# Window mask carried inside the score products of the last stage, instead of by products of its own

## The reference, cut to what matters

```
q, k = l2norm(q) * qs, l2norm(k) * ksc      # then rotary tables are applied
# a window of 32 queries sees 64 keys: the window before, and its own
mask = (it < jb) | (it > jb + w) | (jb == -1)
sim  = einsum('bhwie,bhwje->bhwij', bq, bk2) * QK_SCALE
sim  = where(mask, -finfo.max, sim)
out  = einsum('bhwij,bhwje->bhwie', softmax(sim), bv2)
```

## Time and profile before

| | |
|---|---|
| median of 3 runs | 4238.78 us (4233.77 to 4241.29) |
| the profiled execution | 4246.35 us, its span 4244.5 us |
| PE busy | 92% of the span, 48128 products |
| DVE busy | 83% |
| ACT busy | 62% |
| POOL busy | 56% (it has little to do before the last stage) |
| DMA engines | 24% |
| granted TensorE clock, mean | 0.964 of full speed |

### The profile page before, as it was taken

The page is one execution under the profiler, slowest core; times in us unless marked ns, Lnnn a source line. Parts: engine busy times, 40 slices in busy tenths (PEclk is TensorE's granted clock), DMA queues, the critical chain, the costliest instruction groups (busy, mean ns, idle before and its releaser), DMA issues.

```text
span 4244.5 us, 120128 instructions
## 1 busy us (share of the span) xinstructions
PE 3910.8 (92%) x48128; PEld 2747.8 (65%) x48128; DVE 3529.0 (83%) x5537; ACT 2638.6 (62%) x5550; POOL 2381.6 (56%) x2045
## 2 busy tenths in 40 slices
PE   3457999999995999999999999999999999999998
PEld 1225776767764676667766676667766676667666
DVE  6875556777776899989998899989998899989897
ACT  3543336666664666666667666666666666666665
POOL 0111001000003787878888788878888787878785
PEclk7678999999997999999999999999999999999999
DMA  3000000000001333333332333333332333333332
GB/s 104 0 0 1 1 1 1 1 0 0 0 1 40 76 90 82 69 76 88 78 78 65 79 88 81 70 75 94 73 81 62 81 87 81 71 73 72 91 77 65
DMA packets 264482, 238.94 MB, mean 56 GB/s; under 512 B 31524, under 2 KB 260136, under 8 KB 263208
## 3 DMA queue, kind: packets, MB, share of 16 engines
q1 hardware_dynamic: 263976, 231.82, 23.5%
HBM read 26.20 MB, written 4.19 MB: 7 GB/s over the span
## 4 chain that ended last, share of the span: by engine, by line
PE 73%; DVE 12%; ACT 7%; issue 3%; SPq 2%; POOL 1%; DMA 1%; DVEq 0%; ACTq 0%; POOLq 0%
PE bank L1977 14%; PE bank L1910 13%; PE bank L1995 8%; PE bank L1950 7%; PE bank L2037 5%; PE bank L854 5%; ACT arena L1129 3%; PE bank L2050 2%; PE bank L1943 2%; DVE arena L1016 2%; PE bank L1921 2%; DVE arena L1026 2%; PE bank L1254 1%; SPq L2151 1%; PE bank L1245 1%
## 5 line engine op out<-in xcount | busy, mean ns | idle before, releaser
L1448 DVE TENSOR_TENSOR arena<-bank,tab 128x1024 f32<-128x1024 f32 x768 | 935.5, 1219 | 193.0 <-ACT arena L1680 138.8
L1835 POOL TENSOR_TENSOR arena<-arena 128x512 f32<-128x512 f32 x768 | 1010.7, 1332 | 49.6 <-DMA arena<-arena 44.9
L1680 ACT ACTIVATE arena<-bank 128x512 f32<-128x512 f32 x768 | 457.9, 596 | 538.9 <-PE bank L1910 530.1
L1977 PE MATMUL bank<-m_vo,arena 128*32 128x512 f32 x6144 | 757.9, 599 | 17.4 <-DVE arena L1541 11.1
L1910 PE MATMUL bank<-x_split,wqk_split 128*128 128x256 f32 x4608 | 720.7, 299 | 34.9 <-DVE arena L1448 21.0
L1910 PEld LDWEIGHTS bank<-x_split,wqk_split 128*128 128x128 f32 x4608 | 605.6, 192 | 184.3 <-issue 93.9
L1843 POOL TENSOR_TENSOR arena<-arena 128x256 f32<-128x256 f32 x768 | 558.6, 739 | 159.4 <-ACT arena L1680 158.7
L1704 ACT ACTIVATE arena<-bank 128x512 f32<-128x512 f32 x768 | 456.8, 596 | 186.9 <-PE bank L1977 184.2
L1852 POOL TENSOR_TENSOR arena<-arena 128x1024 f32<-128x1024 f32 x192 | 372.4, 1940 | 263.2 <-DVE arena L1496 263.2
L1187 POOL TENSOR_TENSOR x_all<-x_all,arena 128x256 f32<-128x256 f32 x16 | 11.6, 727 | 836.5 <-DVE arena L1008 836.5
L1858 POOL TENSOR_TENSOR arena<-arena 128x1024 f32<-128x1024 f32 x192 | 373.5, 1946 | 127.0 <-DVE arena L1509 126.7
(11 more groups left out here) (258 smaller groups left out, 7159.4 us busy)
## 6 DMA issues: line engine op xcount, KB each, us to landing
arena<-arena SPq DMA_DIRECT2D x1536, 128.0 KB, 2.5
wqk_stage<-in_wqk SPq DMA_DIRECT2D x6, 1024.0 KB, 8.6
out_x<-x_all SPq DMA_DIRECT2D x7, 512.0 KB, 6.0
wvt<-in_wvt SPq DMA_DIRECT2D x6, 512.0 KB, 4.4
wo<-in_wo SPq DMA_DIRECT2D x6, 512.0 KB, 5.5
arena<-in_wbh SPq DMA_DIRECT2D x1, 2048.0 KB, 9.7
w<-in_w SPq DMA_DIRECT2D x6, 341.0 KB, 5.9
wqk_stage<-out_x SPq DMA_DIRECT2D x2, 512.0 KB, 5.0
```

The lines of the kernel that those rows point to most:

```text
L1448: nc.vector.tensor_tensor(d_t[c % KS].rearrange("p k h t -> p k (h t)"), bank[c % 2][:, :].unsqueeze(1).to_broadcast([P, 2, 2 * T]), tab[: ...
L1680: nc.scalar.activation(d_sq[i % 4].rearrange("p h t -> p (h t)"), bank[c % 2][:, :], ACT.Square).then_inc(s_sq, 1)
L1835: nc.gpsimd.tensor_tensor(d_rot[i // 4][:, i % 4, :, :], t[:, :, 0, :], t[:, :, 1, :], ALU.add).then_inc(s_ad, 1)
L1977: last = nc.tensor.matmul(bank[U_BANK[w]][g * WIN:(g + 1) * WIN, :], d_xt[n % 3][:, w * WIN:(w + 1) * WIN], m_vo[:, 4 * g:4 * g + 4, :].re ...
```

## The change

It takes the mask products away and puts the mask where the zeros of the keys and the unused half of the queries were. `d_q` gets one more axis, `d_q[:, a, g, z, t]`: the 64 partitions of head `z` hold its queries, and the other 64 hold an identity repeated over the tokens (one-hot rows). In `d_k[:, a, g, z, t]` the 64 partitions that were zero hold rows of the mask. A product over all 128 partitions then gives scores plus mask, but it now serves one head alone, so each product of 128 columns becomes two of 64 columns, each with weights of its own.

- `scores`: for each bank 32 products of 64 columns, `start=True`; no products with `mask_bf`; for the first sequence one more wait, on `s_sel`.
- `mask_rows_d`, new, at the start of GpSimd's last stage: the two memsets that were there, and ten copies that write the one-hot rows and the mask rows, each waited for. PE and ACT no longer wait for these memsets before their loops (`ZEROS` 5 instead of 7). `place_keys` waits for all twelve.
- The four VectorE copies that made `ident_bf` and `mask_bf` at the start of the program go. The mask is loaded into `mask_rows`, which stays.
- `place_queries`: the same eight DMAs, to another address.
- `d_q` has twice its size. For this `d_wf` shares memory with `d_v`, and `d_xc` with `d_r`, and `ffn_square` waits for `s_xc` of the sequence before.

```
-        d_q = ld(2, 4, T)
+        d_q = ld(2, 4, 2, T)
...
-        d_xf, d_v, d_r, d_wf, d_xc, d_xn = ld(T), ld(T), ld(T), ld(T), ld(T), ld(T)
+        d_xf, d_v, d_r, d_xn = ld(T), ld(T), ld(T), ld(T)
+        d_wf, d_xc = d_v, d_r
...
-        ZEROS = 7
+        ZEROS = 5
...
+        def mask_rows_d(pool):
+
+            link = Chain(pool, s_sel, 0, 0)
+            link.n = SELS
+            link(nc.gpsimd.memset(d_k, 0.0))
+            link(nc.gpsimd.memset(d_u[:, 0], 0.0))
+            for z in range(2):
+                rows = slice((1 - z) * DH, (2 - z) * DH)
+                for a in range(2):
+                    link(nc.gpsimd.tensor_copy(d_q[rows, a, :, z, :].rearrange("p g (m t) -> p g m t", m=4),
+                                               ident[rows, rows].unsqueeze(1).unsqueeze(1).to_broadcast([DH, 4, 4, DH])))
+                keys = d_k.rearrange("p a g z t -> p (a g) z t")[:, :, z, :]
+                even, later = slice((1 - z) * DH, (1 - z) * DH + WIN), slice((1 - z) * DH + WIN, (2 - z) * DH)
+                link(nc.gpsimd.tensor_copy(keys[even, :, 0:2 * WIN],
+                                           mask_rows[even, 0, :].unsqueeze(1).to_broadcast([WIN, 8, 2 * WIN])))
...
                 act.wait_ge(s_mean, n + 1)
                 at_least(act, s_var, n)
+                at_least(act, s_xc, n)
...
-            nc.gpsimd.memset(d_k, 0.0).then_inc(s_zero, 1)
-            nc.gpsimd.memset(d_u[:, 0], 0.0).then_inc(s_zero, 1)
+            mask_rows_d(pool)
...
                 at_least(pe, s_sub, 2 * n + h)
+                if n == 0 and h == 0:
+                    pe.wait_ge(s_sel, SELS + MASKS)
                 for b in range(2):
-                    for g in range(4):
-                        nc.tensor.matmul(bank[2 + b][g * WIN:(g + 1) * WIN, :], ident_bf[:, g * WIN:(g + 1) * WIN],
-                                         mask_bf[:, min(h + b, 1), :, :].rearrange("p a k -> p (a k)"),
-                                         start=True, stop=True, skip_group_check=True, tile_position=(0, g * WIN))
                     for v in range(2):
                         at = (4 * h + 2 * b + v) * WIN
                         for a in range(2):
-                            for g in range(4):
-                                last = nc.tensor.matmul(bank[2 + b][g * WIN:(g + 1) * WIN, (2 * v + a) * P:(2 * v + a + 1) * P],
-                                                        d_q[:, a, g, at:at + WIN], d_k[:, a, g, :, at:at + 2 * WIN],
-                                                        start=False, stop=True, skip_group_check=True, tile_position=(0, g * WIN))
+                            for z in range(2):
+                                to = ((2 * v + a) * 2 + z) * 2 * WIN
+                                for g in range(4):
+                                    last = nc.tensor.matmul(bank[2 + b][g * WIN:(g + 1) * WIN, to:to + 2 * WIN],
+                                                            d_q[:, a, g, z, at:at + WIN], d_k[:, a, g, z, at:at + 2 * WIN],
+                                                            start=True, stop=True, skip_group_check=True, tile_position=(0, g * WIN))
...
             sp.wait_ge(s_mR, 2 * n + 2)
+            sp.wait_ge(s_sel, SELS + MASKS)
             at_least(sp, s_s, 2 * n)
...
-                    sp.dma_start(d_q[at:at + WIN, r // 2, :, :], d_rot[1][r * WIN:(r + 1) * WIN, :, h, :]).then_inc(s_dq, 16)
+                    sp.dma_start(d_q[at:at + WIN, r // 2, :, r % 2, :], d_rot[1][r * WIN:(r + 1) * WIN, :, h, :]).then_inc(s_dq, 16)
```

More of the change, by code:

```diff
@@ L67, in end @@
         assert self.n == self.per_step, (self.n, self.per_step)
-LOADS_A, LOADS_B, LOADS_C, LOADS_CONST, CONSTS = 3, 4, 5, 10, 7
+LOADS_A, LOADS_B, LOADS_C, LOADS_CONST, CONSTS = 3, 4, 5, 10, 3
 PHASES = 4
@@ L86, in build @@
         ident = sb("ident", [P, P])
-        ident_bf = sb("ident_bf", [P, P], BF16)
-        mask_bf = sb("mask_bf", [P, TPS, 8, 2 * WIN], BF16)
+        mask_rows = sb("mask_rows", [P, TPS, 2 * WIN])
         ones_row = sb("ones_row", [1, P])
@@ L107, in build @@
         qk_cols = sb("qk_cols", [P, 6])
-        ARENA = 30300
+        ARENA = 30560
         WEIGHTS_B_AT = (4 * PAIRS + 1 + 8 + HB) * C + 8
@@ L176, in build @@
         const_ready = sem("const_ready")
-        mask_stage = wqk_stage[:, 0:TPS * 2 * WIN].rearrange("p (t k) -> p t k", t=TPS)
         rope = tab[:, 0, 0, :, :].rearrange("p h (t d) -> p h t d", t=4)
@@ L1400, in build @@
         SELS = 13
+        MASKS = 12
+        def mask_rows_d(pool):
[12 more added lines that the diff above has]
+                                           mask_rows[even, 0, :].unsqueeze(1).to_broadcast([WIN, 8, 2 * WIN])))
+                link(nc.gpsimd.tensor_copy(keys[even, :, 2 * WIN:T].rearrange("p s (m t) -> p s m t", m=3),
+                                           mask_rows[even, 1, :].unsqueeze(1).unsqueeze(1).to_broadcast([WIN, 8, 3, 2 * WIN])))
+                link(nc.gpsimd.tensor_copy(keys[later, :, WIN:].rearrange("p s (m t) -> p s m t", m=4),
+                                           mask_rows[later, 1, :].unsqueeze(1).unsqueeze(1).to_broadcast([WIN, 8, 4, 2 * WIN])))
         def split_high(i):
@@ L2170, in _ @@
             sp.dma_start(wcv, dram["wcv"].rearrange("(b p) c -> p b c", p=P)).then_inc(loaded_a, 16)
-            sp.dma_start(mask_stage[:, 1, :], dram["mask"][1]).then_inc(loaded_const, 16)
+            sp.dma_start(mask_rows[:, 1, :], dram["mask"][1]).then_inc(loaded_const, 16)
             for w in range(WPT):
-                sp.dma_start(mask_stage[w * WIN:(w + 1) * WIN, 0, :], dram["mask"][0][0:WIN]).then_inc(loaded_const, 16)
+                sp.dma_start(mask_rows[w * WIN:(w + 1) * WIN, 0, :], dram["mask"][0][0:WIN]).then_inc(loaded_const, 16)
             for k in range(4):
@@ L2232, in _ @@
             dve.wait_ge(loaded_const, LOADS_CONST * 16)
-            nc.vector.tensor_copy(ident_bf[:, :], ident[:, :]).then_inc(const_ready, 1)
-            for t, at, many in ((1, 0, 8), (0, 4, 4)):
-                nc.vector.tensor_copy(mask_bf[:, t, at:at + many, :], mask_stage[:, 1, :].unsqueeze(1).to_broadcast([P, many, 2 * WIN]))\
-                    .then_inc(const_ready, 1)
-            nc.vector.tensor_copy(mask_bf[:, 0, 0:4, :], mask_stage[:, 0, :].unsqueeze(1).to_broadcast([P, 4, 2 * WIN]))\
-                .then_inc(const_ready, 1)
             nc.vector.memset(ones_row[:, :], 1.0).then_inc(const_ready, 1)
```

## The result

The changed kernel takes 4304.98 us (median of four runs, 4304.8 to 4315.7), beside 4240.03 us for the kernel before in the same series: a ratio of 1.0161 (1.0148 to 1.0173), 65 us slower. The forecast was 4166 us, with 4262 as the end of the range. Both were missed, and by a way that the prediction had seen as a question and answered wrongly: how fast PE gets its instructions.

The account below looks back on a forecast made before the run. PE was taken to bound the last stage, 96 turns, with DVE close behind. Passes -78, handback +6 and constants -0.9 gave -73 us, so 4166 us against the median 4238.78; range 4152 to 4262.

Parts of the forecast that it names:

- The price of a 64-column pass: PE in `scores`: 14 ns a pass, 56 ns for four, a call 1.79 us instead of 2.19, 78 us less in all.
- The two objections on weight loads: PE in `scores`: loads of 110 ns, or 27 ns each one after another, could hold up passes; both set aside.
- The rate of instructions: PE in `scores`: eight instructions per 56 ns, 7 ns each, taken as possible from a burst at under 4 ns; left unclosed.
- passes don't get shorter: Rival, PE in `scores`: load and product pairs stay at one in 27.2 ns; +248 us, 4487 us; chance 0.20.
- Part of the way: Rival, PE in `scores`: a pace of 16 to 18 ns a pass; -27 to +22 us, 4212 to 4261; chance 0.06.
- The handback: Last stage's turns: some handovers with DVE touch, so 0.06 us a turn is lost, 6 us, between 0 and 15.
- a projection block that comes 0.80 us too early: PE at 2992.08 would come at 2991.28, but needs DVE's split tokens, done at 2991.69; fits only if DVE moves up.
- handed back: Rival, last stage: DVE or GpSimd's wait for keys ends last; first call's 38 us stay, second's go; 4200 us; chance 0.12.
- The copies: GpSimd at the last stage's start: ten copies end between 1328 and 1334.3, up to 4 us late; cost 0, at most 4.
- The cover that I named (DVE's 7.42 us): Last stage's start: DVE normalises for 7.42 us from 1334.14 while PE waits until 1342.83, covering late GpSimd copies.
- Constants, keys, SyncE, added waits: DVE's four start copies gone, -0.9 us; keys' way doesn't bind; SyncE's same eight DMAs, 0; ScalarE's wait for `s_xc`, 0.

Follow-up runs that it names:

- e1: Kernel before, each mask product of 512 columns made eight of 64, each clearing its bank, score products unchanged: 4298.15 us beside 4237.72, ratio 1.0141.
- e10: Kernel before without its mask products and no mask in their place: 4188.14 us beside 4237.09, ratio 0.9887.
- e9: Kernel before with each mask product in four pieces of 128 columns, only the first clearing the bank: 4248.22 us, ratio 1.0022.

## Why the prediction was wrong, step by step

**The price of a 64-column pass: right.** I went by the nearest rows to 14 ns a pass, and a call to 1.79 us. Measured are 13.9 ns at best and 1.81 us a call in the turn shown. The two objections on weight loads were rightly set aside: 128 loads of 110 ns each lie within 1.81 us, so they overlap.

**The rate of instructions: the step that failed.** I wrote "this is the point that I can't close", put this term of the sum at nothing and gave the forecast a chance of 0.62 all the same. It measured 101 us of standstills. The evidence was a burst of 12 instructions at under 4 ns in the earlier trace rows. The burst was true of the burst: e1's mask passes run at 0.24 us / 64 = 3.75 ns an instruction. What it could not show is how long PE can be fed at that pace. The trace could have: the standstill at 1972.65 in the earlier trace rows was itself one for "issue", with 0.47 us of idle time before it, in a row of attention products. I used it as a stopwatch for the loads and didn't ask what PE had waited for. The page's line of fetches gave 256 instructions a piece. That standstill, too, lies at the piece's edge, at the same place modulo 256. And the earlier trace rows had 440 passes in a turn, to which the change adds 112. The pace of before was near the limit already: at 13.6 ns an instruction, the pace of its score products, 256 last 3.5 us, and a piece comes at best every 3.2 us.

**The rival "passes don't get shorter": right in its sign, wrong in its mechanism.** It put a limit of instructions into each pass, at 27.2 ns, and a price of 248 us. Its rate was close: a piece every 3.2 us is 25 ns for a load and its product. But PE meets the limit only when the piece in hand is used up. A pass takes 14 ns, and the limit shows as 0.2 to 3 us of nothing at a piece's edge, most of it in the second call and in the `attention` behind it, a block that I had left alone. "Part of the way" assumed a uniform pace as well and isn't what happened, though its 4212 to 4261 us lies nearest. The rule of the Trainium skill, page TensorE: Matmul & The Clock Gate, section Back-to-back issue gap, a floor of about 25 ns for 1 to 64 columns, doesn't hold over four tiles: the row has 13.9 ns for a pass. Within one tile a pass comes every 56 ns, above the floor.

**The handback: too small.** Taken were 6 us with 15 as the worst. In the changed kernel a second call takes 1.81 us in the median, a first call 2.04. By the table of blocks `scores` should have lost 78 us and gained 6; without 62 us more of standstills it lost 56, so 22 were handed back in the score blocks alone. e10 has 37 of 86 in all. In the sum I looked for a projection block that comes 0.80 us too early; the first call's 0.33 us in e10 already go in the step right behind it. The rival "handed back" had 40 of 78 us lost, which is nearly what e10 shows. It named the second call, though, and the loss shown is in the first.

**The copies: right that they are done in time, wrong that they cost nothing.** The cover that I named (DVE's 7.42 us) hides a late GpSimd. It doesn't hide that DVE itself gets slower while GpSimd copies. About 4 us, the end of my range, by another way than I had in mind.

**Constants, keys, SyncE, added waits: right** as far as one can tell; together they were put at a microsecond, and nothing in the waits speaks of them.

The sum anew, from what was measured: -78 for the passes; +101 of standstills (109 less 8); +22 handed back in the score blocks; +4 for the start; -1 for the constants. This gives +48, where the medians show +65. Some 17 us are not assigned. About 11 of them lie in `attention`, which grew by 48 with 37 of standstills; what they are isn't shown.

**What stays open.** Half of the standstills' time (45 of 88 us between 1700 and 4150 us) lies behind pieces that were used up in under 3.3 us. The other half lies behind longer pieces; there the fetch started 1.4 to 6.3 us after PE had entered the piece ahead. Why those fetches started late no run here tells. Before has late ones as well, but its shortest piece lasts 3.7 us, and only two of its steps in `scores` and `attention` are over 0.2 us. No fetch starts for 14 us or more in 49 places of the changed kernel's last stage, but 35 of these hold no score pass at all: there 256 instructions simply last that long. The 730 instructions between two fetches in my expectation of e9 are wrong: the trace of before has at most 432, that of the changed kernel 494. No experiment changed how the pieces are fetched, and of the dose only three points are known.

## What to carry to other kernels

Before splitting products, count instructions in the densest stretch as well as columns, loads included, and ask how long any 256 in a row will last. Here a kernel whose quickest 256 last 3.7 us went through, and kernels with 67 to 86 such pieces under 3.3 us lost some 50 to 100 us to standstills. Read the fetch line of the page and every wait for "issue" inside a row of equal products, since a kernel that already has one is near the edge. And take time off a full engine's block only after looking at what the very next block waits for: of 86 us of mask products, only 49 were to be had.

## What the runs showed of the hardware

- **Instructions come in pieces of 16384 bytes, 256 for PE**, and 106 of 117 standstills end at one place modulo 256. The Trainium skill, page Runtime: NRT & Kernel Launch, section Instruction fetch mechanics, has the same size of a block, and the trace agrees with it. The section also holds that fetching is hidden behind the pace at which instructions are issued. Here it isn't: 109 us of the changed kernel's last stage are such standstills.
- **PE has little more than one piece in hand**: fetches start at least 3.2 us apart, take 0.9 to 1.8 us in the changed kernel, and PE goes on 1.2 to 1.6 us after the landing. None starts while PE has over 300 instructions to go before it reaches the new piece.
- **The pace of issue isn't the limit**: 64 instructions in 0.24 us, 3.75 ns each, in e1, and 256 in 1.81 us, 7.1 ns each, in the changed kernel.
- **Four column tiles share the time**: one pass of 64 columns in f32 takes 13.9 ns in the mean, four tiles side by side in 56 ns; at 128 columns it is 109 ns.
- **A GpSimd copy holds up DVE**: two normalisations take 3.15 us beside copies and 0.60 without, while DVE's memsets (1.09 us in both) don't mind. The Trainium skill, page SBUF — State Buffer, section SBUF: two separate sides, has a pair of ports that the two engines share and that one of them blocks for its whole instruction. The rows fit that: DVE's row at 1314.71 ends at 1317.86, long enough for the whole copy of 1.89 us that began at 1314.79 to lie in it. Which operation waited for which, the rows don't resolve.
